# Sixty-four routed experts: the slots as stationary operand on the way up, and the gated rows turned for the way down

## What is computed

```
xb = jnp.zeros((E, CAP, D), xf.dtype).at[se, pos].set(xf[tok], mode='drop')
h = jax.nn.silu(jnp.einsum('ecd,eid->eci', xb, w1)) * jnp.einsum('ecd,eid->eci', xb, w3)
yb = jnp.einsum('eci,edi->ecd', h, w2)
valid = (pos < CAP).astype(xf.dtype)
contrib = yb[se, jnp.minimum(pos, CAP - 1)]
wf = weights.reshape(-1)[order] * valid
y = jnp.zeros_like(xf).at[tok].add(contrib * wf[:, None])
```

## Time and profile before

| what | us |
|---|---|
| median of three runs | 4219.72 |
| lowest and highest run | 4213.58, 4223.89 |
| the profiled execution, its own time | 4223.3 |
| its span | 4221.5 |
| start of the first transfer of `l1_slots` in the span | 1727.17 |
| start of its last indirect transfer | 1802.63 |
| start of the first transfer of the next phase | 1809.77 |

### The profile page before, as it was taken

One profiled execution on the slowest core, in us unless ns is written; L12 is line 12 of the kernel. 1 busy time (PEld: TensorE's weight loads), 2 busy tenths in 40 slices (PEclk: granted clock), 3 DMA queues, 4 the chain that ended last, 5 costly groups with the idle time before them and its releaser, 6 DMA issues. The chain is left out here.

```text
span 4221.5 us, 75199 instructions
## 1 busy us (share of the span) xinstructions
PE 3238.3 (77%) x24864; PEld 2435.1 (58%) x24865; DVE 2707.6 (64%) x8110; ACT 1874.4 (44%) x5363; POOL 734.9 (17%) x958
## 2 busy tenths in 40 slices
PE   3568469466665888686778867999899997886897
PEld 3446359433333665475556654666577776665786
DVE  6546643468885777257985544555477775557997
ACT  1346334133332665234874433222255554445886
POOL 0045533200002677442000210000100000000000
PEclk9879679768885666587886777999899999998999
DMA  4040057400003000333000012333200000000000
GB/s 121 1 173 0 28 165 235 130 1 1 0 0 141 23 0 1 102 122 103 0 0 0 1 40 65 101 100 99 75 1 0 0 0 4 0 0 16 1 0 20
DMA packets 136026, 197.22 MB, mean 47 GB/s; under 512 B 25017, under 2 KB 91119, under 8 KB 134125
## 3 DMA queue, kind: packets, MB, share of 16 engines
q1 hardware_dynamic: 124357, 186.31, 14.3%
q0 software_dynamic: 11520, 9.05, 0.7%
HBM read 151.49 MB, written 58.63 MB: 50 GB/s over the span
## 5 line engine op out<-in xcount | busy, mean ns | idle before, releaser
L2715 ACT ACTIVATE l_ffn_sg<-l_ffn_p_g 128x512 f32<-128x512 f32 x168 | 100.3, 597 | 355.0 <-PE l_ffn_p_g L2752 355.0
L2686 DVE TENSOR_TENSOR l_ffn_part<-l_ffn_sg,l_ffn_share 128x512 f32<-128x512 f32 x168 | 116.4, 693 | 190.3 <-ACT l_ffn_sg L2715 183.2
L2742 PEld LDWEIGHTS l_ffn_p_o<-l_ffn_wd,l_ffn_h 128*128 128x128 f32 x1344 | 175.7, 191 | 85.0 <-issue 76.1
L109 POOL TENSOR_TENSOR rstd<-vareps,minus_half 128x4 f32<-128x4 f32 x10 | 10.4, 1044 | 1164.3 <-DVE vareps L88 1164.3
L1508 POOL DMA_INDIRECT slots_in<-l_xattn_x,l_xattn_slot x192 | 190.3, 991 | 82.9 <-issue 49.9
L2881 ACT ACTIVATE l_attn_E<-l_attn_p_s,l_attn_nm 128x128 f32<-128x128 f32 x512 | 181.3, 386 | 2.9 <-DVE l_attn_nm L2839 2.9
L2742 PE MATMUL l_ffn_p_o<-l_ffn_wd,l_ffn_h 128*128 128x128 f32 x1344 | 178.0, 275 | 2.2 <-DVE l_ffn_h L2689 1.6
L2752 PE MATMUL l_ffn_p_g<-l_ffn_f_xTall,l_ffn_wg 128*128 (+1 forms) x336 | 173.5, 598 | 0.5 <-DVE l_ffn_turned L2677 0.5
L2754 PE MATMUL l_ffn_p_u<-l_ffn_f_xTall,l_ffn_wu 128*128 (+1 forms) x336 | 172.5, 595 | 0.0
L2898 PEld LDWEIGHTS l_attn_p_y<-l_attn_xT,l_attn_wqkv 128*128 128x128 f32 x1024 | 131.3, 194 | 34.1 <-issue 32.7
L2898 PE MATMUL l_attn_p_y<-l_attn_xT,l_attn_wqkv 128*128 128x128 f32 x1024 | 137.3, 278 | 1.6 <-DVE l_attn_qT L2843 1.5
(11 more groups left out here) (827 smaller groups left out, 9644.9 us busy)
## 6 DMA issues: line engine op xcount, KB each, us to landing
l_experts_w<-in_L_ffn_w SPq DMA_DIRECT2D x72, 512.0 KB
l_ffn_share<-share_rows SPq DMA_DIRECT2D x112, 256.0 KB, 3.2
slots_in<-l_xattn_empty SPq DMA_DIRECT2D x8, 2145.0 KB, 24.2
shares_out<-l_xattn_zero SPq DMA_DIRECT2D x24, 512.0 KB, 10.7
l_out_got<-shares_out SPq DMA_DIRECT2D x16, 768.0 KB, 4.5
l_attn_toep<-kernel_rows SPq DMA_DIRECT2D x1, 8192.0 KB, 30.9
xattn_toep<-ssm_rows SPq DMA_DIRECT2D x1, 8192.0 KB, 32.0
l_slots_w<-in_L_ffn_w SPq DMA_DIRECT2D x32, 176.0 KB
```

Of the source, the lines that this page charges most:

```text
L2686: dve.tensor_tensor(part[:, w], sg[:, w], share[:, slot], ALU.mult).then_inc(s.share_used, 1)
L2715: act.activation(sg[:, k], p_g[:, k], ACT.Silu).then_inc(s.silu_ready, 1)
L2742: mm = pe.matmul(p_o[:, u, q * P:(q + 1) * P], h[:, (u * CH + c) % 2, q * P:(q + 1) * P], wd[:, c], start=(c == 0 and q == 0), stop=(c == ...
```

## The change

On the way up the operands change places. The 64 slots of an expert (`xT`, 128 x 64) are now stationary, and the expert's weights of gate and up part together (128 x 176) move. The result is 64 slots by 176, and as on the way down the first expert's lands in partitions 0 to 63 and the second's in 64 to 127 of `p_h`. So there are two multiplications per pair where there were four. The silu and the product now run over 128 partitions by 88 instead of 88 partitions by 128.

The way down needs the product with the inner width in the partitions. So PE transposes `h` (new tile `p_t`), and DVE copies it to `hT` (new tile, 88 x 128), which takes the place of `h` as stationary operand of the way down.

The new step has its own place in the pipeline. PE's item t is now: transposition of the slots of t, transposition of `h` of t - 2, hidden values of t - 1, way down of t - 3. ACT scales t - 3. DVE's item t is: copy of `hT` of t - 2, product of t - 1, meta of t. The way down of a pair, and all that waits for it, stands one item later than before. SP's and POOL's programs are the same, with the same number of buffers.

```diff
-        xT, sg, h, y = sb("xT", [P, 2, P]), sb("sg", [FP, 2, P]), sb("h", [FP, 2, P]), sb("y", [P, V, P])
-        p_x, p_h, p_y = ps("p_x", [P, 2, 512]), ps("p_h", [P, 2, 512]), ps("p_y", [P, 2, 512])
+        xT, sg, h, hT, y = sb("xT", [P, 2, P]), sb("sg", [P, 2, FP]), sb("h", [P, 2, FP]), sb("hT", [FP, 2, P]), sb("y", [P, V, P])
+        p_x, p_h, p_t, p_y = ps("p_x", [P, 2, 512]), ps("p_h", [P, 2, 512]), ps("p_t", [P, 2, 512]), ps("p_y", [P, 2, 512])
...
             def _(act):
-                for item in written_out(2, NP, V):
+                for item in written_out(3, NP, V):
                     for n, u in item(1):
                         act.wait_ge(s.hid_psum, n + 1)
-                        act.activation(sg[:, n % 2], p_h[0:FP, n % 2, 0:P], ACT.Silu).then_inc(s.silu_ready, 1)
+                        act.activation(sg[:, n % 2], p_h[:, n % 2, 0:FP], ACT.Silu).then_inc(s.silu_ready, 1)
...
-                    for n, u in item(2):
+                    for n, u in item(3):
                         act.wait_ge(s.y_psum, n + 1)
...
             def _(dve):
-                for item in written_out(1, NP, V):
+                for item in written_out(2, NP, V):
+                    for n, u in item(2):
+                        dve.wait_ge(s.hT_psum, n + 1)
+                        after(dve, s.y_psum, n - 1)
+                        dve.tensor_copy(hT[:, n % 2], p_t[0:FP, n % 2, 0:P]).then_inc(s.hT_ready, 1)
                     for n, u in item(1):
                         dve.wait_ge(s.silu_ready, n + 1)
-                        after(dve, s.y_psum, n - 1)
-                        dve.tensor_tensor(h[:, n % 2], sg[:, n % 2], p_h[0:FP, n % 2, P:2 * P], ALU.mult).then_inc(s.h_ready, 1)
+                        after(dve, s.hT_psum, n - 1)
+                        dve.tensor_tensor(h[:, n % 2], sg[:, n % 2], p_h[:, n % 2, FP:2 * FP], ALU.mult).then_inc(s.h_ready, 1)
...
             def _(pe):
-                for item in written_out(2, NP, V):
+                for item in written_out(3, NP, V):
...
+                    for n, u in item(2):
+                        pe.wait_ge(s.h_ready, n + 1)
+                        after(pe, s.hT_ready, n - 1)
+                        pe.transpose(p_t[0:FP, n % 2, 0:P], h[:, n % 2], R.ident[:]).then_inc(s.hT_psum, 1)
                     for n, u in item(1):
...
-                        for g in range(2):
-                            for e in range(2):
-                                w = (2 * e + g) * FP
-                                mm = pe.matmul(p_h[0:FP, n % 2, g * P + e * CAP:g * P + (e + 1) * CAP], w13[:, u, w:w + FP],
-                                               xT[:, n % 2, e * CAP:(e + 1) * CAP], start=True, stop=True)
+                        for e in range(2):
+                            mm = pe.matmul(p_h[e * CAP:(e + 1) * CAP, n % 2, 0:2 * FP], xT[:, n % 2, e * CAP:(e + 1) * CAP],
+                                           w13[:, u, 2 * e * FP:2 * (e + 1) * FP], start=True, stop=True)
                         mm.then_inc(s.hid_psum, 1)
-                    for n, u in item(2):
-                        pe.wait_ge(s.h_ready, n + 1)
+                    for n, u in item(3):
+                        pe.wait_ge(s.hT_ready, n + 1)
                         pe.wait_ge(down_in[u], (n // V + 1) * DMA)
```

More of the change, by code:

```diff
@@ L1889, in l1_slots @@
     NP, TARGETS = E // 2, NB * P * 6
-    with phase(nc, "l1_slots", "x0 x1 x2 x3 up0 up1 up2 up3 down0 down1 down2 down3 xT_psum xT_ready meta_ready hid_psum silu_ready h_ready y_psum y_ready") as (s, sb, ps):
+    with phase(nc, "l1_slots", "x0 x1 x2 x3 up0 up1 up2 up3 down0 down1 down2 down3 xT_psum xT_ready meta_ready hid_psum silu_ready h_ready hT_psum hT_ready y_psum y_ready") as (s, sb, ps):
         x, w13, w2 = sb("x", [P, V, D + 2]), sb("w13", [P, V, 4 * FP]), sb("w2", [FP, V, 2 * P])
         to, part = sb("to", [P, V, 1], U32), sb("part", [P, V, 1])
-        xT, sg, h, y = sb("xT", [P, 2, P]), sb("sg", [FP, 2, P]), sb("h", [FP, 2, P]), sb("y", [P, V, P])
-        p_x, p_h, p_y = ps("p_x", [P, 2, 512]), ps("p_h", [P, 2, 512]), ps("p_y", [P, 2, 512])
+        xT, sg, h, hT, y = sb("xT", [P, 2, P]), sb("sg", [P, 2, FP]), sb("h", [P, 2, FP]), sb("hT", [FP, 2, P]), sb("y", [P, V, P])
+        p_x, p_h, p_t, p_y = ps("p_x", [P, 2, 512]), ps("p_h", [P, 2, 512]), ps("p_t", [P, 2, 512]), ps("p_y", [P, 2, 512])
         x_in, up_in, down_in = [s.x0, s.x1, s.x2, s.x3], [s.up0, s.up1, s.up2, s.up3], [s.down0, s.down1, s.down2, s.down3]
@@ L1969, in _ @@
                         for e in range(2):
-                            mm = pe.matmul(p_y[e * CAP:(e + 1) * CAP, n % 2, 0:P], h[:, n % 2, e * CAP:(e + 1) * CAP], w2[:, u, e * P:(e + 1) * P],
+                            mm = pe.matmul(p_y[e * CAP:(e + 1) * CAP, n % 2, 0:P], hT[:, n % 2, e * CAP:(e + 1) * CAP], w2[:, u, e * P:(e + 1) * P],
                                            start=True, stop=True)
```

## The result

The changed kernel takes 4229.5 us in the median of 20 runs (4225.2 to 4239.1), the kernel before 4221.9 in the median of 20 (4213.6 to 4228.6). The ratio is 1.0019, with a 95% interval of 1.0012 to 1.0026: 5 to 11 us slower, 7.6 by the medians, within the 0.3% that count as no change. The profiled execution took 4232.9, its span is 4231.1.

A forecast was written before the change was run, and what follows sets the result against it. The prediction took PE at 1.2 GHz to bound the phase before, and x queued behind w2 on SP after. Items +1.6, fill and drain +1.5, late landings +4 gave 4219.7 + 7 = 4227 us, range 4214 to 4239.

The forecast's parts named there:

- x behind w2 becomes the bound: SP's queue: w2 waits one item longer for a way down, delaying x; PE waits 0.3 us per item.
- What would show it: Signs listed for the changed trace: hidden values 0.70 us, intervals alternating 2.0 and 2.6, first to last way down over 70.
- PE's work per item, 1.98: PE at 1.2 GHz: 0.27 + 0.39 + 0.70 + 0.62 = 1.98 us per item against 2.17; bounds 1.75 and 2.2.
- Do two experts run side by side with 128 rows: Hidden values on PE: both experts run at the same time in array halves, 0.70 us instead of 1.28.
- that rival: Hidden values on PE: experts run one after the other, PE's work 2.68 us per item, program 4236; chance 0.08.
- The loop through x, 2.30 per item: Way down, SP's issue, landing of x, next item but one's way down: 4.61 us for two items, 2.30 each.
- Late landings, +4: Late x and indirect transfers now reach the time: four times 1 us, +4; bounds +1 and +7.
- Fill +1.1, drain +0.4: Phase's ends: the additional item before the first way down costs 1.1 us, transposition and copy between the last two 0.4.
- The sum: Whole phase: items +1.6, fill and drain +1.5, late landings +4, together +7 us.
- The first rival, the array's work counts: Landing of x stays hidden and PE's work sets the phase's pace: -6 us, 4214; chance 0.08.
- The third rival, the clock: PE's granted clock rises in the phase: 1.8 us per item, -7 us, 4213; chance 0.04.

The follow-up runs named there:

- the repetition: The changed kernel, unedited, measured again on another chip beside the kernel before: 4227.4 us against 4218.4, ratio 1.0017.
- the kernel with the late w2: Kernel before the change, with only SP's wait ahead of w2 made one item later: 4229.0 us, 1.0024 of the kernel before.
- the fivefold one: The changed kernel with its phase run five times in one program: 4584.4 us, 87.3 us per phase.
- the fivefold programs: Kernel before and changed kernel, each with the phase run five times in one program: 4560.4 and 4584.4 us.
- both loops opened: Changed kernel with SP issuing w2 behind the next pair's x and w13, and DVE's meta one item later: 4211.8 us, 0.9986 of the kernel before.
- both edits: Changed kernel with w2 issued behind the next pair's x and w13, and DVE's meta one item later; here with the phase five times: 4515.4 us.
- the fivefold kernel before: The kernel before the change with its phase run five times in one program: 4560.4 us, 82.2 us per phase.

## Why the prediction held, step by step

- **That x behind w2 becomes the bound: right**, shown from both sides: taking the wait out of x's way takes the loss away, and moving the wait alone makes it in the old kernel. PE waits at the transposition of slots, released by `x`, w2's issue stands right after a way down and x's behind it, and DVE waits for `shares_out`, as "What would show it" has them. Three of its signs came less clean. The row of four records is busy 0.85 us, not 0.70, since it overlaps the way down (from its start to the way down's are 0.64). The intervals don't alternate between 2.0 and 2.6; most lie between 1.8 and 2.5, with the mean about right. And from the first way down to the last are 68.2 us (1738.83 to 1807.03; 67.1 in the repetition), where "over 70" was forecast and 65.9 was before.
- **PE's work per item, 1.98: too high by 0.13.** In the timeline above: slots to transposition of `h` 0.27 as predicted; from there to the hidden values 0.37 (0.39); hidden values 0.64 (0.70); way down 0.57 (0.62, "unchanged"). The last was taken over from before and changed. A likely reason, not tested by itself: both multiplications now have the same layout of halves, and the weight loads of the way down begin 0.30 ahead of it (1766.29, 1766.59). In the old order they begin together with it, at 1763.49 in the kernel with the late w2 above. The prediction had priced only the step into the way down, at the end of the hidden values.
- **Do two experts run side by side with 128 rows: right.** Four records of 528 ns each lie in 0.85. One after the other they would have taken 1.40, and that rival fell with this row.
- **The loop through x, 2.30 per item: 2.24.** Way down to issue of `x` 1.09 (1.15 predicted), landing 2.1 in the median as before, and 1.85 - 0.57 = 1.28 to the way down (1.36): 4.47 for two items. The median landing is the same as in the earlier trace rows; the row of the changed kernel for 1740:1790 is

```profile
DMA to landing us min/median/max: 1.8/2.1/3.4
```

  (Such a row counts only the transfers whose landing the trace holds. In the earlier trace rows that is 12 of the 23 in 1740:1790, so "the quickest of 23" was the quickest of 12.)

- **Late landings, +4: too high by about 1.** In the single program two of the 31 intervals are over 3 us (3.64, 3.49), in the fivefold one two or three of each phase, up to 4.26. The mean item there is 2.34, 0.10 above the loop's 2.24: 2.8 us in 28 items. The timeline bears that out: from the seventh item of a phase on, `x` is used 2.32 us after its issue in the mean and 2.09 in the median, and half of the difference is 0.11 per item. Mechanism right, its term too large.
- **Fill +1.1, drain +0.4: +0.94 and +0.92.** The first way down starts at 1738.83, 6.85 after the first transposition, where it was 5.91. At the other end the last transposition of slots is at 1801.78 and the last way down ends at 1807.68; 5.90 where it was 4.98. The prediction's 0.4 counted the work between the last two ways down only, not the whole stage that the last pair has to go through.

```profile
1731.98 0.47 PE L1958 MATMUL l_slots_p_x<-ident,l_slots_x 128*128 128x128 f32 x1 [30.41 <-DMA l_slots_x<-slots_in]
...
1738.83 0.64 PE L1976 MATMUL l_slots_p_y<-l_slots_w,l_slots_hT 88*64 88x128 f32 x4
...
1801.78 0.47 PE L1958 MATMUL l_slots_p_x<-ident,l_slots_x 128*128 128x128 f32 x1 [0.48 <-DMA l_slots_x<-slots_in]
...
1806.54 1.14 PE L1976 MATMUL l_slots_p_y<-l_slots_w,l_slots_hT 88*64 88x128 f32 x8
```

- **The sum.** With the measured terms 28 x 2.34 - 62.8 + 1.9 = +4.6 per phase. One term is missing in it and in the prediction's sum: the fill is counted up to a way down, the items from a transposition, and the way down now stands 1.28 behind its item's start instead of 1.54, which adds 0.3. (29 x 2.17 is also 62.9, not 62.8.) That makes +4.7, and the fivefold programs give 4.8, their profiles 5.1. The predicted +7.1 lies some 2.4 over it: 1.7 from the loop (28 x 0.06) and 1.2 from late landings, less the 0.4 that fill and drain are more, and the missing term. The other 3 us of the 7.6 have no term; nothing here shows whether they are more than scatter. So the mechanism is the prediction's merit; that +7 meets 7.6 so closely is in part luck. The forecast for the phase was 2.4 us too high, and the programs differ by some 3 us that aren't the phase's.
- **The first rival, the array's work counts**, did not come, for the reason given: no `x` whose landing the traces hold took 1.45 us or less. Its -6 was too small by the 0.13 per item of PE's work: 28 x 1.85 - 62.8 + 1.9 = -9.1, and with both loops opened the phase is 8.2 shorter in the single program and 9.0 per phase in the fivefold one.
- **The third rival, the clock**: 0.50 in every stretch of the phase in the changed kernel, 0.84 for 5 us (1775 to 1780) in its repetition. See the last section.

The Trainium skill, TensorEngine Tiling (Array Packing), Key Properties, says that a change of the tiling mode drains TensorE. The trace agrees: the weight loads of the hidden values, the first in halves behind a whole-array transposition, are held back 10.2 us in 32 items, 0.32 each. The same page's Performance Considerations recommend the swap with 2x column tiling, and its Overview, Theoretical Speedup, gives up to 2x where a dimension is 64 or less. The hidden values went from 1.28 to 0.64, but tiling alone is not shown to be worth 2x: by the 0.105 per 64 columns of the earlier trace rows, streaming alone would have gone from 0.84 (eight records) to 0.58 (two pairs of 176 columns), a gain of 0.26. The rest is the 0.44 above streaming that eight short records had, with the change of layout behind them, against 0.06 now.

## What to carry to other kernels

A stage added to a software pipeline makes every step behind it let go of its buffers one item later. Before adding it, look at every queue that issues in order for a wait on such a buffer, and at what unrelated load stands behind it; give that tile one more buffer or issue the load first. When several engines wait at once, the size of a row of waits doesn't say what its removal brings (here taking away 177 us of it brought nothing, and the same edit 6.4 us or more per phase once `x` was no longer late): open the loop that is longest per item first, and keep the other edit for when it has become the bound. To find a few us in thousands, run the phase several times in one program, with its counterpart on the same chip.

## What the hardware showed that was not expected

**The clock can rise in this phase.** In the kernel before, run five times over, all 40 stretches of 10 us read 0.50. With the change and both edits it is 0.50 in the first phase (74.3 us from its first transposition to the next phase's, where the kernel before takes 82.6, so the gain is not the clock's), but higher in 13 of the 36 stretches after 1735, most of all here:

```profile
1992.00:1996.00 4.00, 4.00 (x25) 2.44 (x24) 1.30 (x8) 1.56 (x6) 2.23 (x3) 0.50 0.69 185
1996.00:2000.00 4.00, 3.51 (x25) 1.92 (x23) 1.64 (x10) 2.20 (x9) 2.17 (x3) 0.74 0.64 171
2000.00:2004.00 4.00, 3.02 (x30) 1.98 (x30) 1.84 (x11) 1.45 (x6) 2.25 (x3) 1.00 0.73 199
```

PE had been busy 4.00 of 4.00 us at 0.50 in the stretches ahead. At the full clock (2.4 GHz) its items are still 1.5 to 2.2 us apart, since it waits for `x` and `hT` again:

```profile
2001.55 0.33 PE L1963 MATMUL l_slots_p_x<-ident,l_slots_x 128*128 128x128 f32 x1 [0.49 <-DVE l_slots_hT L1946]
...
2004.94 0.33 PE L1963 MATMUL l_slots_p_x<-ident,l_slots_x 128*128 128x128 f32 x1 [0.69 <-DMA l_slots_x<-slots_in]
```

The prediction gave 1.8 per item to its third rival, but for the changed kernel without these edits, so this is no test of it. With the change alone or one edit it rises in 1 to 3 of some 40 stretches. What makes it rise in one phase and not in the next was not tried, and stays open. The Trainium skill, TensorE: Matmul & The Clock Gate, Why this matters for your kernels, would have a TensorE that works without a pause at the full clock. Here PE is at half of it while busy 10.00 of 10.00 us, and in all 40 stretches of the fivefold kernel before, 27 of which (counted from 1740 on) are busy 10.00 of 10.00 too, so the trace does not agree.

**Landings of `x` are late now and then**: in the ten profiles that hold such times the median is 2.0 to 2.3 us and the longest 3.2 to 4.2, with the same transfers. Whether that costs anything depends on the reserve: the kernel before swallows nearly all of them (in the fivefold one, from the fifth item of a phase on, one interval in all is over 2.25), the changed one shows two or three intervals over 3 us per phase.

**An indirect transfer took 2.9 and 3.0 us** in the two pairs measured, from POOL's issue until the engine that waits for it goes on, against 2.1 in the median for the direct load of `x`.
